# Edge messages in blocks of 128 edges with a segment sum of two levels, in a kernel of two graph layers

## The reference, cut to what matters

```python
x = h[src] + edge_rel_emb               # 40000 x 256, h is the layer norm of the nodes
hid = relu(x @ W1 + b1)
msg = hid @ W2 + b2
agg = segment_sum(msg, dst, num_segments=2500)
return h + agg
```

## Time and profile before

| | us |
|---|---|
| median of 3 runs | 1974.48 (1974.3 to 1975.52) |
| the profiled execution | 1974.99 |
| its span, first to last instruction | 1973.3 |
| PE busy / DVE / ACT / POOL | 1493.3 / 855.8 / 456.7 / 733.1 |
| first gather of the edge stage starts at | 850.52 |
| last gather starts at | 1410.34 |

### The profile page before, as it was taken

One profiled execution on the slowest core, in us unless ns is written; L12 is line 12 of the kernel. 1 busy time (PEld: TensorE's weight loads), 2 busy tenths in 40 slices (PEclk: granted clock), 3 DMA queues, 4 the chain that ended last, 5 costly groups with the idle time before them and its releaser, 6 DMA issues. The chain is left out here.

```text
span 1973.3 us, 25612 instructions
## 1 busy us (share of the span) xinstructions
PE 1493.3 (76%) x7518; PEld 1063.7 (54%) x7519; DVE 855.8 (43%) x2466; ACT 456.7 (23%) x872; POOL 733.1 (37%) x789
## 2 busy tenths in 40 slices
PE   1999998747810883568889888888796789439998
PEld 1566668234610773457667676666555633116665
DVE  4799981774530234523333333333387900201111
ACT  1355550102100331111111111111142233011221
POOL 1111100273246342057777777777613000221111
PEclk9999999767755897789999999999897989769999
DMA  3730000300222345055555555555300070141120
GB/s 67 180 100 1 2 2 2 76 0 8 62 82 78 96 113 121 31 160 152 146 145 148 146 146 146 145 147 147 103 0 1 1 213 0 40 107 44 47 58 10
DMA packets 125356, 161.58 MB, mean 82 GB/s; under 512 B 50879, under 2 KB 93357, under 8 KB 125012
## 3 DMA queue, kind: packets, MB, share of 16 engines
q1 hardware_dynamic: 64973, 100.89, 18.3%
q0 software_dynamic: 60288, 59.51, 12.1%
HBM read 125.85 MB, written 36.05 MB: 82 GB/s over the span
## 5 line engine op out<-in xcount | busy, mean ns | idle before, releaser
L1579 POOL DMA_INDIRECT em_gathered<-edge_table,em_which x320 | 395.0, 1234 | 145.9 <-POOL em_which L1575 72.7
L1599 PE MATMUL em_projected<-em_w,em_attr 128*125 128x256 f32 x1280 | 308.6, 390 | 62.7 <-DVE em_pre L1646 38.7
L1599 PEld LDWEIGHTS em_projected<-em_w,em_attr 128*125 128x125 f32 x1280 | 241.5, 192 | 116.9 <-DVE em_pre L1646 52.3
L1606 PE MATMUL em_total<-em_hidden,em_hot 125*125 125x256 f32 x792 | 196.6, 397 | 33.0 <-DVE em_hot L1657 19.0
L1704 ACT ACTIVATE em_hidden<-em_pre 125x512 f32<-125x512 f32 x160 | 100.8, 630 | 500.0 <-DVE em_pre L1646 456.9
L1646 DVE TENSOR_TENSOR em_pre<-em_projected,em_gathered 125x512 f32<-125x512 f32 x160 | 110.3, 690 | 241.0 <-DMA em_gathered<-edge_table,em_which 236.7
L1606 PEld LDWEIGHTS em_total<-em_hidden,em_hot 125*125 125x125 f32 x792 | 150.3, 195 | 74.9 <-issue 52.8
L2112 PE MATMUL oe_up<-xn_T,oe_w 128*128 128x500 f32 x384 | 168.3, 598 | 10.8 <-DMA oe_b<-in_ffn_b_T 7.3
L460 DVE TENSOR_SCALAR nm_hot_key<-nm_key_order,nm_key_now 125x500 bf16<-125x500 int16 x500 | 172.2, 344 | 0.0
L504 PE MATMUL nm_acc<-nm_hot_key,nm_hot_a 125*125 125x500 bf16 x500 | 161.4, 399 | 0.4
L2112 PEld LDWEIGHTS oe_up<-xn_T,oe_w 128*128 128x128 f32 x384 | 74.4, 195 | 98.8 <-issue 89.8
(11 more groups left out here) (367 smaller groups left out, 2311.7 us busy)
## 6 DMA issues: line engine op xcount, KB each, us to landing
em_attr<-in_edge_attr_T SPq DMA_DIRECT2D x80, 500.0 KB
oe_wd<-in_ffn_Wd SPq DMA_DIRECT2D x8, 1024.0 KB, 11.5
best_rows<-blank SPq DMA_DIRECT2D x1, 7041.0 KB
choice_rows<-blank SPq DMA_DIRECT2D x1, 6070.3 KB
mx_rows<-choice_rows SPq DMA_DIRECT2D x12, 453.2 KB
em_gathered<-edge_table,em_which POOLq DMA_INDIRECT x320
state<-in_x SPq DMA_DIRECT2D x2, 2240.0 KB
mx_answer<-mx_answers SPq DMA_DIRECT2D x10, 448.0 KB
```

Of the source, the lines that this page charges most:

```text
L1579: nc.gpsimd.indirect_dma_start(out=gathered[:, v, s, :], out_offset=None, in_=table, in_offset=bass.IndirectOffsetOnAxis(ap=which[:, v, s: ...
L1599: last = nc.tensor.matmul(projected[:, u, k, j, :], attr[:, u, k * TWO + j, f, :], w1[:, f, :], start=(f == 0), stop=(f == KB - 1))
L1606: last = nc.tensor.matmul(total[:, at, 0:DIM], hot[:, at, s, :], hidden[:, u, s, :], start=(s == 0), stop=(s == SUB - 1))
```

## The change

- Edges are padded to 313 blocks of 128 (the last block has 64 edges). Eight blocks are a set (40 sets, the last one with one block), two blocks are a lane of 256 edges.
- Everything in `edge_messages` is unrolled: no loops, no conditionals. POOL's gather takes the source numbers straight from a tile laid out by the host (`edge_src_cols`), so the copy and its wait go. The ring of gathered blocks has 12 places instead of 16. Attributes are loaded by sets of 1 MB in a ring of three.
- The segment sum has two levels. First each lane sums its 256 edges into 32 targets, counted from the lane's lowest target: a matmul with 32 weight columns, whose output stands at partitions 0, 32, 64 or 96 by the lane; four lanes fill one PSUM bank, copied by ACT to `part`. Then each tile of 125 targets is the sum over four sets: four matmuls with a one-hot matrix of 128 partial rows by 125 targets, copied by ACT to `hidden_sum`. DVE no longer adds to `hidden_sum`, and POOL no longer clears it.
- The numbers that this takes (`EdgeLanes`: each lane's lowest target, the first set of each tile) are worked out in `mixture`: three DMAs ahead of SP's weights, seven between the weights and the wait for `sent`, some thirty small DVE instructions before L1445 and three after it, four iotas on POOL. The `row_ranges` work in `EdgeKeys` goes (two DMAs, ten DVE instructions, one matmul, POOL's `earlier_rows`).
- The iota of 2500 numbers goes from `constants`.
- A new stage `general_messages` behind `edge_messages` does the general case (a lane over more than 32 targets, or a tile over more than four sets); its engines read the flag `lanes.wide` and jump over its body otherwise.

```diff
+BLOCKS, SET_BLOCKS, LANE_BLOCKS = -(-EDGES // 128), 8, 2
+LANE, LANES_AT_ONCE = 32, 4
+SETS = -(-BLOCKS // SET_BLOCKS)
+LANES = SETS * LANES_AT_ONCE
+TILE_SETS, LAST_SET = 4, 3
+ATTR_RING = 3
...
-            nc.gpsimd.iota(c.iota_node_i[:], [[1, NODES]], base=0, channel_multiplier=0).then_inc(made, 1)
...
 def mixture(p, c, A, state, x, xn, xn_T, lanes):
                 sp.dma_start(router[:], by_block(A["router_T"])).then_inc(router_loaded, 16)
+                lanes.sync_first(sp)
...
                 sp.wait_ge(router_loaded, 16)
+                lanes.sync_last(sp)
                 sp.wait_ge(sent, TOP * TILES * 16)
...
+                lanes.vector_steps(dve)
                 for n in range(1, TOP):
                     dve.wait_ge(sent, n * TILES * 16)
                     dve.wait_ge(rows_numbered, n)
                     nc.vector.tensor_scalar(state[:, :, NUMBER:ROW], ...)
+                lanes.vector_last(dve)
...
 def edge_messages(p, c, A, lanes, w1, attr, attr_loaded, table, hidden_sum):
             def _(sp):
+                for s in range(ATTR_RING, SETS):
+                    sp.wait_ge(projected_ready, pairs_of(s - ATTR_RING)[-1] + 1)
+                    load_attributes(sp, A, attr, attr_loaded, s)
             def _(pool):
-                    nc.gpsimd.tensor_copy(which[:, v, :], src[:, bass.ds((turn * SETS + v) * SUB, SUB)]).then_inc(copied, 1)
-                    pool.wait_ge(copied, turn * SETS + v + 1)
...
+                nc.gpsimd.iota(order_i[:], [[1, P]], base=0, channel_multiplier=0).then_inc(numbered, 1)
+                for n in range(BLOCKS):
+                    if n >= GATHERED:
+                        pool.wait_ge(pre_ready, (n - GATHERED) // 2 + 1)
+                    nc.gpsimd.indirect_dma_start(
+                        out=gathered[:, n % GATHERED, :], out_offset=None, in_=table, in_offset=bass.IndirectOffsetOnAxis(
+                            ap=lanes.which[:, n:n + 1].bitcast(mybir.dt.uint32), axis=0)).then_inc(got[n % GATHERED], 16)
             def _(pe):
+                def sum_lanes(s):
...
+                    for b in range(LANE_BLOCKS):
+                        for lane in range(LANES_AT_ONCE):
+                            n = lane * LANE_BLOCKS + b
...
+                                last = nc.tensor.matmul(lane_sum[lane * LANE:(lane + 1) * LANE, s % 2, 0:DIM], hot[:, s % 2, n, :],
+                                                        hidden[:, slots(s).start + n, :], start=(b == 0),
+                                                        stop=(b == LANE_BLOCKS - 1 or alone))
+                def sum_tiles(s):
+                    for t in tiles_after(s):
+                        first = pe.value_load(lanes.firsts[0:1, t, 0:1], min_val=0, max_val=SETS - TILE_SETS)
...
+                        for k in range(TILE_SETS):
+                            last = nc.tensor.matmul(total[:, t % 2, 0:DIM], tile_hot[:, t % 2, k, :],
+                                                    part[:, bass.ds(first + k, 1), :].rearrange("p a d -> p (a d)"),
+                                                    start=(k == 0), stop=(k == TILE_SETS - 1))
+                for s in range(SETS):
+                    project(s)
+                    if s >= 1:
+                        sum_lanes(s - 1)
+                    if s >= 2:
+                        sum_tiles(s - 2)
             def _(dve):
+                for s in range(SETS):
...
+                    nc.vector.tensor_tensor(hot[:, s % 2], order[:, 0:LANE].unsqueeze(1).broadcast_to([128, SET_BLOCKS, LANE]), ...)
+                    for k in pairs_of(s):
...
+                        nc.vector.tensor_tensor(pair_slots(k), projected[:, k % BANKS, 0:width, :], gathered[:, at:at + width, :],
+                                                ALU.add).then_inc(pre_ready, 1)
+                    if s >= 1:
+                        tile_hots(s - 1)
             def _(act):
+                        nc.scalar.activation(pair_slots(k), pair_slots(k), ACT.Relu).then_inc(hidden_ready, 1)
...
+                        keep_lanes(s - 1)
```

More of the change, by code:

```diff
@@ L318, in vector_first @@
         nc.vector.tensor_reduce(self.high[:], self.by_block[:], AX.X, ALU.max).then_inc(self.reduced, 1)
[L319 to L335, removed]
+        dve.wait_ge(self.made, 1)
         nc.vector.tensor_copy(self.up[:], self.up_i[:])
@@ L1233, in vector_steps, with mixture @@
         nc.vector.engine_nop().then_inc(self.ready, 1)
-def mixture(p, c, A, state, x, xn, xn_T):
+def mixture(p, c, A, state, x, xn, xn_T, lanes):
     nc = p.nc
@@ L1248, in mixture @@
         way = Dispatch(p, c, scope, "md", TOP)
+        lanes.enter(p, scope)
         SORTED = sorted_tiles(TOP)
@@ L1503, in _ @@
                 sp.wait_ge(stored, 32)
-            @block.gpsimd
-            def _(pool):
-                nc.gpsimd.memset(hidden_sum[:], 0.0)
             @block.tensor
@@ L1540, in edge_messages @@
         sem = lambda n: p.sem("em_" + n)
-        both = lambda name: [sem(f"{name}{u}") for u in range(2)]
-        which = sb("which", [P, SETS, SUB], I32)
-        gathered = sb("gathered", [P, SETS, SUB, DIM])
-        pre = sb("pre", [P, 2, SUB, DIM])
-        hidden = sb("hidden", [P, 2, SUB, DIM])
-        hot = sb("hot", [P, 3, SUB, P])
-        dst_f = sb("dst_f", [P, EDGE_TILES])
-        projected = p.ps("em_projected", [P, 2, BANKS, TWO, DIM], scope=scope)
-        total = p.ps("em_total", [P, 3, 512], scope=scope)
@@ L1559, in load_further @@
-        def load_further(engine, b):
-            return load(engine, b, 2, 0, TILES * RANGE_ROWS)
+        gathered = sb("gathered", [128, GATHERED, DIM])
+        hidden = sb("hidden", [128, HIDDEN_RING * SET_BLOCKS, DIM])
+        order_i, order = sb("order_i", [128, P], I32), sb("order", [128, P])
+        hot = sb("hot", [128, 2, SET_BLOCKS, LANE])
+        tile_hot = sb("tile_hot", [128, 2, TILE_SETS, P])
+        part = sb("part", [128, SETS, DIM])
+        projected = p.ps("em_projected", [128, BANKS, 2, DIM], scope=scope)
@@ L1685, in _, with tile_hots @@
-                nc.vector.tensor_copy(dst_f[:], dst[:]).then_inc(prepared, 1)
-                dve.wait_ge(prepared, 1)
-                dve.sem_inc(added, 2)
-                dve.sem_inc(more_added, 1)
-                combine(0, 0)
-                with dve.Fori(0, TURNS - 1) as turn:
-                    for v in range(SETS):
-                        sums(turn, v, lambda: combine(turn, v + 1) if v + 1 < SETS else combine(turn + 1, 0))
-                for v in range(SETS):
-                    sums(TURNS - 1, v, lambda: v + 1 < SETS and combine(TURNS - 1, v + 1))
+                def tile_hots(s):
+                    for t in tiles_after(s):
+                        first = dve.value_load(lanes.firsts[0:1, t, 0:1], min_val=0, max_val=SETS - TILE_SETS)
+                        if t >= 2:
+                            dve.wait_ge(tile_summed, t - 1)
+                        for k in range(TILE_SETS):
+                            last = nc.vector.tensor_scalar(tile_hot[:, t % 2, k, :], order[:], float(t * P),
+                                                           lanes.row_node[:, bass.ds(first + k, 1)], ALU.add, ALU.is_equal)
+                        last.then_inc(tile_hot_ready, 1)
@@ new lines, in keep_tiles @@
+                def keep_tiles(s):
+                    for t in tiles_after(s):
+                        act.wait_ge(tile_summed, t + 1)
+                        nc.scalar.activation(hidden_sum[:, t, :], total[:, t % 2, 0:DIM], ACT.Copy).then_inc(tile_kept, 1)
+                for s in range(SETS):
+                    for k in pairs_of(s):
+                        act.wait_ge(pre_ready, k + 1)
+                        nc.scalar.activation(pair_slots(k), pair_slots(k), ACT.Relu).then_inc(hidden_ready, 1)
+                    if s >= 1:
+                        keep_lanes(s - 1)
+                    if s >= 2:
+                        keep_tiles(s - 2)
```

463 lines of the change are left out of this document (299 added, 164 removed).

## The result

The changed kernel took 1897.85 us (median of 4 runs, 1890.21 to 1900.5), the kernel before 1975.0 beside it (4 runs): a ratio of 0.9602, 95% interval 0.9573 to 0.9631. The forecast was 1898. The profiled execution took 1900.5 with a span of 1898.7.

What follows compares the result with a forecast made beforehand. POOL's gather issue was taken to bound the edge stage. Edge stage and jump -76.6 us, constants -2.2, mixture's scatters +1, bias +1: -77 from 1974.99 gives 1898 us, range 1883 to 1922.

Steps and rivals of the forecast that it cites:

- The gather term: Edge stage, POOL: 312 steps of 1.225 us a gather plus 0.30 gap, 476.4 us from first to last gather start.
- small surplus for DVE's one-hot work: Edge stage: gathers beside DVE's one-hot work run longer; half the earlier surplus, so 1.225 us a gather instead of 1.215.
- a full lock of the shared port: Edge stage: by the skill's rule DVE blocks POOL for whole instructions, some 23 us more; not in the sum.
- the sign named for "right": Edge stage profile: gathers of 1.21 to 1.24 us with 0.30 between them, 1.53 a step.
- the signs named for "wrong": Edge stage: POOL waiting on DVE's adds, 3 us POOL gaps, gathers over 1.25, PE's clock at 0.5, adds waiting for projection.
- POOL stays the bound: Edge stage: POOL's gather issue sets the pace without stalls; 1898 us, own range 1883 to 1908, chance 0.62.
- PE takes over: Edge stage: PE's 461 us plus 29 for output-width switches passes POOL by 14; 1905 to 1935 us, chance 0.2.
- POOL stalls in unrolled code: Edge stage: one extra 3.3 us in 39 gathers, 8 in 313, +26 us; 1905 to 1924, chance 0.11.
- Slower, lane sums don't pipeline: Edge stage, PE: each lane-sum record costs 0.397 us, PE 568 us; 1990 us, or 2110 with weights unhidden; chance 0.05.
- PE's work: Edge stage: 2038 PE records take 355 us if four lanes run at once, 461 if one after another.
- The constants: Kernel start: removing the 2.21 us iota, which the load at 4.19 waits for, saves 2.2 us.
- The jump: Behind the edge stage: jumping over the new general stage adds 4.5 us, bounds 0.5 to 6.

Runs made afterwards that it cites:

- e5: The changed kernel word for word, measured again with no edit; 1809.53 us, ratio 0.9173.
- e10: The changed kernel with gathers of 128, 127, 126, 125, 124, 120, 112 and 64 rows in turn; 1899.92 us.
- e8: The changed kernel with 125 rows a gather in place of 128, plus a memset of the gathered blocks; 1896.26 us, ratio 0.9611.
- e4: The kernel before with only its 320 gathers of 125 rows unrolled, straight from the index columns without the copy; 1905.91 us, ratio 0.9639.
- e9: The changed kernel word for word, measured a third time with no edit; 1810.49 us.
- e11: The changed kernel with the two loops around the lane sums swapped, so both blocks of a lane follow each other; 1812.08 us.
- e12: The changed kernel without the call of the jumped stage general_messages; 1807.52 us.
- e3: The changed kernel with four attribute buffers, two sets of hidden buffers, and PE's sets 9 to 36 as a loop; 1809.53 us.
- e7: The changed kernel with 100 satisfied waits added to PE's stream at the end of the stage before; 1808.81 us.
- e6: The changed kernel with the hidden ring cut from 3 sets to 2; 1810.06 us.

## Why the prediction was right, and where it was not

**The gather term failed.** The prediction took 1.225 us for 128 rows, from bounds of 1.19 to 1.244, "since transfers of other width differ by 0.02 only", and a step of 1.527. Measured: 0.95 and 1.25, 312 steps 391.7 us in e5, 85 us under the 476.4 of the sum. The bounds failed because all their rows had the same 125 partitions and differed only in bytes and direction; I scaled by rows where rows / k counts (25 to 8, e10). With 125 rows the sum holds: 476.4 forecast, 473.6 in e8, and 1896.26 us. Its small surplus for DVE's one-hot work was sized by a mechanism that the traces bear out: in e4 and e5 only gathers beside that work are over 0.05 us longer than usual. It was forecast at 0.010 us a gather and came to 0.002 in e8 (mean 1.213 against the usual 1.211). The 23 us that a full lock of the shared port would have cost are not there.

**The recorded time agrees by accident.** In the first measurement PE received instructions too slowly in the edge stage and then ran at the lower clock, and POOL waited some 76 us for it (467.6 against 391.7). That filled the gap left by the mis-sized term to within a few us: 476.4 in the sum, 467.6 measured, the stage's tail 6.6 longer than in e5. The forecast was right in its time by luck. A time that fits doesn't confirm the mechanism: gathers of 1.21 to 1.24 were the sign named for "right" and took 0.95, and of the signs named for "wrong" two stood in the profile, POOL waiting for DVE's adds and the adds waiting for the projection.

**What bounds the stage.** "POOL stays the bound" is right for e5, e9 and e8, wrong for the recorded run. The rival *PE takes over* named the right engine for that run and the wrong reason: its 29 us for the switches were more than twice too many. In the three rows of e5 under e11, the two projection records, 16 lane records and two projection records take 1056.70 to 1058.93, 2.23 us; seven slots of 0.216 (the spacing of projections there) and one record of 0.38 would be 1.89. So both switches of a set together cost some 0.34 us, 13 us in 39 sets. *POOL stalls in unrolled code*: none in 313 gathers; the odd gap before the last of the mixture's 40 indirect DMAs (3.62 before) stands there again in the first measurement and in e5 (3.61), so it belongs to that place. *Slower, lane sums don't pipeline*: no; 626 records were busy for 43 to 47 us.

**PE's work.** Forecast 355 us if four lanes run at once, 461 if not. Measured 369.9 in e5 over the whole stage: the first case and the 13 us of switches, 368. It matters more than the prediction saw: at 461, PE and not POOL would bound a stage whose gathers need 391.

**The other terms.** The constants: -2.19 against -2.2 forecast. The jump: +5.1 (e12) against +4.5, inside the bounds of 0.5 to 6. From the last gather's start to the next stage's first load 18.8 us were forecast; 18.9 came in e8 and 19.2 in e5. EdgeKeys, mixture and the bias: forecast 0, +1 and +1; the first gather stood at 850.58 where 850.1 was forecast, at 847.7 and 849.1 in e5 and e9, so what is left of these terms is under the scatter of that landmark. Of the mixture one can see more: from its first indirect DMA to its last (569.34 to 634.15 before) it takes 0.65 us longer in the first measurement and 0.4 in e5, where +1 was forecast. The bias landed for DVE at 822.34.

**What each part brings**, on the later occasions: 1975 to 1906 by straight gathers (e4), to 1896 by the rest of the change at the same 125 rows (e8), to 1810 by 128 rows (e5). The last step was in no term of the sum. It should need the one before it, since in e4 PE is already busy for 94 of 100 us; no run tries 128 rows with the one-level sum.

**Open.** Why PE was fed slowly in the first measurement. Excluded as sufficient causes by runs: the unrolled code, its DMA load and its rings (e5 and e9 are the same kernel without stretches). Not excluded: something about that single occasion, outside the kernel, alone or together with the unrolled code. The kernel before, whose PE stream loops in this stage, took 1975.0 beside it and 1973.5 to 1976.2 later, so it felt nothing of it. The later measurements ran on three chips, e5 and e9 on two of them; on which the first ran isn't on record.

The traces keep one more thing that bears on it, the transfers of the instructions themselves. Those of 16 KB must be PE's code, since e3 has none between 972 and 1226 us, where PE loops, and e5 has 10 there. The first measurement has 17 of them between 850 and 1340 us, of 0.93 to 1.63 us each; e5 has as many up to 1250, of 0.94 to 2.16. So they were no longer than usual, and none is near as long as a stretch: the longest stretch begins at 868.4, the nearest transfer at 874.36, with 1.13 us. They come about every 258 PE records and the stretches about every 328. When a transfer was asked for isn't in the trace, so this speaks against slow transfers of code and doesn't settle the matter. Code placement (e7) and the hidden ring (e6) couldn't be tested, since the stretches didn't return in any of the ten further runs with this stage unrolled. So 1897.85 is what was recorded, 1809.5 to 1810.5 is what two repetitions gave, and no later run reproduces the first.

## What to carry to other kernels

Price an indirect DMA on GpSimd by rows / k (k being the largest divisor of the row count up to 16), not by rows or bytes: 128 rows cost 0.95 us and 125 cost 1.21. When a bound comes from rows of the trace, check that these rows differ in the dimension that the change alters. And repeat the unchanged kernel beside the experiments: here that control, and no edit, showed that the change alone doesn't make the slow stretches.

## What the runs showed of the hardware that was not expected

- Issue of an indirect DMA takes 0.91 us for 64 rows, 0.96 for 128, 1.00 for 126, 1.20 for 125, 1.29 for 124 and 2.55 for 127, each with 0.30 behind it.
- Four strips of 32 columns run at once, the records of a group of four starting 7 ns apart, 16 records in 1.07 us where 16 on the full array take 3.62, and still in 1.09 us when both blocks of a strip follow each other.
- PE can be fed one instruction per 0.7 us for up to some 18 us in code that it otherwise runs at about 0.22 us a record, with no wait named in the profile. The clock was 1.00 as this began (868 to 873 us, 7 matmul records) and 0.50 behind it (874 to 890). Over the whole stage it cost 46.0 us of longer busy time and 39.4 of standing still against e5.
- A switch of PE from 128 to 32 output columns and back costs some 0.34 us for both ways (e5).
- With POOL as a slower bound (e8) PE is busy for 82 of 100 us and the granted clock was 0.95; with PE busy for 93 in e5 it was 0.98.
- Gathers are stretched only beside DVE's one-hot work, whose inputs both lie in SBUF: by up to 0.5 us in e4, where that work is 65.6 us and the gathers grow by 9 us in all, and by up to 0.24 in e5, 1.5 us in all.
